# Waits between the gathers and the scatters that GpSimd issues in a routed expert layer

## The reference, cut to what matters

```python
xn = _layernorm(x, axis=-1)
x = x + attn_ref(xn, ...) + ffn_ref(xn, Wr, W1, W2)
...
# attn_ref: causal conv over 4 taps, two sigmoid gates, h = a*h + b along the sequence,
# a projection with W_out, and a root-mean-square norm
...
# ffn_ref: t = 4096 tokens, E = 8 experts, cap = 512 tokens each
eidx = jnp.argmax(probs, axis=-1)
...
keep = rank < cap
...
xe = xf[dispatch]
h = jnp.maximum(jnp.einsum('ecd,edf->ecf', xe, W1), 0.0)
ye = jnp.einsum('ecf,efd->ecd', h, W2)
ye = ye * (pe * valid)[:, :, None]
y = zeros.at[dispatch.reshape(-1)].add(ye.reshape(E * cap, d))
```

## Time and profile before

| what | us |
|---|---|
| median of 3 runs (lowest to highest) | 166.86 (165.87 to 166.94) |
| the profiled execution's own time | 165.59 |
| span of the profiled execution | 163.8 |
| POOL busy, of that in L350 and in L357 | 83.2, 32.1 and 37.1 |
| PE busy, DVE busy, ACT busy | 124.8, 93.5, 86.2 |

### The profile page before, as it was taken

The page is one execution under the profiler, slowest core; times in us unless marked ns, Lnnn a source line. Parts: engine busy times, 40 slices in busy tenths (PEclk is TensorE's granted clock), DMA queues, the critical chain, the costliest instruction groups (busy, mean ns, idle before and its releaser), DMA issues.

```text
span 163.8 us, 2058 instructions
## 1 busy us (share of the span) xinstructions
PE 124.8 (76%) x684; PEld 98.2 (60%) x684; DVE 93.5 (57%) x207; ACT 86.2 (53%) x197; POOL 83.2 (51%) x102
## 2 busy tenths in 40 slices
PE   5966999999995991699999739896979967941000
PEld 5956999836533890439659318694968956930000
DVE  4179300399898000861512410768948999299990
ACT  3047625014554840648685363999608958635650
POOL 7069640000477774377477876377765807560000
PEclk9997555579999999569999999999999999999555
DMA  4898699970011211011011111011110100116997
GB/s 133 231 270 315 268 356 342 399 318 2 16 48 36 54 58 48 18 49 49 16 52 48 48 48 48 16 50 49 49 46 21 33 16 32 42 58 183 327 301 214
DMA packets 14346, 19.27 MB, mean 118 GB/s; under 512 B 1664, under 2 KB 10112, under 8 KB 14336
## 3 DMA queue, kind: packets, MB, share of 16 engines
q1 hardware_dynamic: 9888, 13.63, 24.5%
q0 software_dynamic: 2048, 4.20, 8.7%
q10 hardware_dynamic: 2400, 1.32, 3.0%
HBM read 10.76 MB, written 8.39 MB: 117 GB/s over the span
## 4 chain that ended last, share of the span: by engine, by line
PE 40%; DVE 24%; DMA 8%; issue 8%; ACT 7%; another core or an unknown queue 6%; POOL 3%; POOLq 1%; SPq 0%; DVEq 0%; ACTq 0%
PE bank L495 8%; PE bank L427 7%; PE bank L385 7%; DVE xnT L869 5%; DMA x_tok<-in_x 4%; PE bank L395 4%; DVE xc L838 4%; PE bank L482 3%; DVE inp L865 3%; PE bank L416 3%; PE bank L484 2%; PE bank L483 2%; DVE dec L922 2%; DMA dec<-y_rows 2%
## 5 line engine op out<-in xcount | busy, mean ns | idle before, releaser
L357 POOL DMA_INDIRECT y_rows<-xn_tok,idx_out x32 | 37.1, 1159 | 25.2 <-DVE xn_tok L876 15.9
L350 POOL DMA_INDIRECT xn_tok<-xn_rows,idx_in x32 | 32.1, 1002 | 29.9 <-DVE idx_out L801 20.4
L618 ACT ACTIVATE h_sb<-bank 128x512 f32<-128x512 f32 x32 | 18.1, 596 | 25.7 <-PE bank L484 16.8
L495 PE MATMUL bank<-w_raw,h_sb 128*128 128x128 f32 x256 | 30.2, 275 | 0.1
L495 PEld LDWEIGHTS bank<-w_raw,h_sb 128*128 128x128 f32 x256 | 29.2, 192 | 0.2 <-issue 0.2
L482 PE MATMUL bank<-xg_hi,w_hi 128*128 128x512 f32 x32 | 14.0, 437 | 12.0 <-ACT h_sb L618 5.4
L427 PE MATMUL bank<-xc,par 128*128 128x512 f32 x32 | 17.2, 670 | 3.0 <-issue 2.8
L845 DVE TENSOR_TENSOR xg_lo<-bank,xg_hi 128x512 fp32r<-128x512 f32 x8 | 5.5, 688 | 18.6 <-ACT xg_hi L612 14.2
L876 DVE COPY xn_tok<-bank 128x512 f32<-128x512 f32 x7 | 4.8, 684 | 18.2 <-remote 11.3
L482 PEld LDWEIGHTS bank<-xg_hi,w_hi 128*128 128x128 f32 x32 | 6.1, 191 | 14.9 <-ACT h_sb L618 6.8
L427 PEld LDWEIGHTS bank<-xc,par 128*128 128x128 f32 x32 | 6.6, 214 | 12.0 <-issue 11.0
(11 more groups left out here) (111 smaller groups left out, 211.8 us busy)
## 6 DMA issues: line engine op xcount, KB each, us to landing
w_raw<-in_weights SPq DMA_DIRECT2D x8, 512.0 KB, 7.5
y_rows<-sca SPq DMA_DIRECT2D x4, 512.0 KB, 5.8
dec<-y_rows SPq DMA_DIRECT2D x8, 256.0 KB, 5.0
x_tok<-in_x SPq DMA_DIRECT2D x3, 512.0 KB, 9.4
xn_rows<-xn_tok SPq DMA_DIRECT2D x3, 512.0 KB, 3.5
out<-dec SPq DMA_DIRECT2D x4, 256.0 KB, 3.0
out<-dec ACTq DMA_DIRECT2D x4, 256.0 KB, 3.2
x_tok<-in_x SPq DMA_DIRECT2D x2, 256.0 KB, 5.4
```

The lines of the kernel that those rows point to most:

```text
L350: g.indirect_dma_start(gathered[:, s * D:(s + 1) * D], None, xn_rows, bass.IndirectOffsetOnAxis(ap=idx_in[:, s:s + 1], axis=0)).then_inc(g ...
L357: g.indirect_dma_start(y_rows, bass.IndirectOffsetOnAxis(ap=idx_out[:, s:s + 1], axis=0), gathered[:, s * D:(s + 1) * D], None).then_inc(s ...
L495: last = mm(tile_of(e, s), h_sb[:, k * CAP + s * P:k * CAP + (s + 1) * P], w_raw[:, e, F + k * D:F + (k + 1) * D], start=(k == 0), stop=(k ...
L618: a(h_sb[:, k * CAP:(k + 1) * CAP], hbank[n % 3][:, :], ACT.Relu).then_inc(h_done, 1)
```

## The change

GpSimd gets two waits in its loop over the experts. Ahead of each scatter it waits until the gather that it issued last has landed. Ahead of each gather in the loop it waits until all scatters so far have landed.

```diff
             pool.wait_ge(idx_done, 2)
             pool.wait_ge(zero_out, 16 * C)
+
             for e in range(E):
+                pool.wait_ge(gather_in[min(e + AHEAD, E) - 1], 16 * ST)
                 scatter(e)
                 if e + AHEAD < E:
+                    pool.wait_ge(scattered, 16 * ST * (e + 1))
                     gather(e + AHEAD)
```

## The result

The changed kernel took 168.3 us (167.7 to 169.9, 4 runs) beside 166.4 us of the kernel before: a ratio of 1.014, with a 95% interval of 1.010 to 1.019. It is slower by over 1%, inside the stated range but not in its likeliest case. The profiled execution took 168.28 us, with a span of 166.5. The chips turned out to be of two sorts: in three comparisons, this one included, the kernel before takes some 166 us, and in two, on two other chips, some 150.5 us.

What follows compares the result with a forecast made beforehand. PE (40% of the chain) and DVE (24%) set the end, POOL only 3%. Landings of 5.2 + 6.4 = 11.6 us fit into 12.0 us of room, so nothing is added: 166.9 us, range 164.7 to 170.2.

Steps and rivals of the forecast that it cites:

- likeliest case: The added waits stay hidden in GpSimd's idle time: 166.9 us, own range 166.0 to 168.2, chance 0.66.
- The cost of a turnaround: Ahead of gathers 4 to 7 and scatters 1 to 4: 1.30 us per scatter landing, 1.6 per gather landing, 11.6 in all.
- the upper bound for it: Gather 4's landing: DMA engines still move rows until 2.24 us after its descriptors are done; 1.6 us was taken.
- The room, and the walk through the loop: GpSimd's waits for DVE inside the loop leave 12.0 us to spend; start times forecast from gather 4 (74.6) to scatter 6 (135.6).
- slow stretch: Time in the chain without a known releaser while other engines stand still: 7.01 us from 59.12, 2.68 us from 120.65.
- Who waits for the later gathers: Gather 7 lands by 122.5, PE's transposes of it run at 126.74: 4.2 us of cover, more for gathers 4 to 6.
- PE's L469 should not wait for a gather: Sign in the profile after: PE's transposes of gathered rows are held by no gather.
- the start of scatter 7: Sign at the last expert: scatter 7 starts within 1 us of 141.7; after 143 the forecast is wrong.
- The rival that landings are longer: At the eight turnarounds, a surplus comes back eightfold: 0.5 us each gives 169.9 us; chance 0.24, other hold-ups included.
- The rival that stretches shrink: Waits break up the second stretch, at most 2.7 us: 164.2 us; with issue time at 94.38 gone too, 161.4; chance 0.10.
- The tail: SP's loads of `y_rows` behind scatter 7: the first 0.65 us of lateness are hidden, reserve about 1 us, beyond it all counts.
- theory C: From the experiments' expectations: PE's slow stretches set the end whatever the gathers do; 168 to 171 us for the early gather near 166.

Runs made afterwards that it cites:

- scatter_waits: The changed kernel with only the waits ahead of gathers 4 to 7: 156.21 us beside 150.67, ratio 1.037; again 155.75 us beside 150.29, ratio 1.036.
- gather_waits: The changed kernel with only the waits ahead of scatters, for the gather issued last: 157.8 us beside 150.67 of the kernel before, ratio 1.049.
- gather7_early: The changed kernel, both waits kept, but gather 7 right behind gather 6, ahead of scatter 3: 160.15 us beside 150.67 of the kernel before, ratio 1.064.
- gather7_early_no_waits: The kernel before, no added wait, but gather 7 right behind gather 6, ahead of scatter 3: 150.66 us beside 150.29, ratio 1.001.
- gather7_early_again: The changed kernel with gather 7 right behind gather 6, on another chip: 165.0 us beside 165.99 of the kernel before, ratio 0.998.

## Why the prediction was right, and where it was wrong

- **The cost of a turnaround.** Right. Forecast were 5.2 + 6.4 = 11.6 us on top of the usual 0.3 us gaps. Measured were 6.3 + 8.1 - 8 x 0.3 = 12.0 us: 1.27 us for a scatter's landing (1.30 taken) and 1.72 for a gather's (1.6 taken). The widest, gather 4's, took 2.54 - 0.30 = 2.24 us, as the upper bound for it had said. On the chips near 150.5 the total time puts 1.4 us on each, which includes that fewer DMAs were held up.
- **The room, and the walk through the loop.** Right for the profile it was read from, and POOL came to the last expert early. But the room of 12.0 us was taken as a property of the kernel. It depends on the chip: in four profiles from the other sort of chip (`scatter_waits`, `gather_waits`, `gather7_early`, `gather7_early_no_waits`), none with a slow stretch in its chain, GpSimd never waited for DVE longer than 0.3 us, so the room was zero. That the stretches make the room is argued from this, and from DVE's evictions coming 5.9 to 15.0 us earlier without them; no run takes them away and leaves the rest as it was.
- **Who waits for the later gathers.** This is the step that failed. I set gather 7's landing, forecast for 122.5, against PE's transposes at 126.74, and called the difference 4.2 us of cover. But 126.74 was where PE came because of slow stretches ahead of it, which I had named as a rival and left out of this step. In the changed kernel PE was there at 120.5, 2.0 us ahead of even the forecast landing, and the landing, 2.2 us later than forecast (the hold-ups of scatter 3), came at 124.67. A cover of 4.2 us became a stand of 4.2 us, followed by a lower clock that cost 2.4 us more. The sign that PE's L469 should not wait for a gather failed, and so did the start of scatter 7, at 144.30 instead of within 1 us of 141.7. `gather7_early_again` supports that this is the loss: without the stand it took 165.0 us, against 170.27 on the same chip. The evidence is not complete, as that kernel also has two turnarounds fewer and its twin without waits ran on the other sort of chip only.
- **The rival that landings are longer.** Its direction came true, not its mechanism: the landings were as forecast, and PE's wait for a gather ended last, not GpSimd's work. The upper end of the range, 170.2, was set by this rival, so that the range took the measured time in is in part luck.
- **The rival that stretches shrink.** Its first half came true: the stretch behind 120 and the issue time at 94 went, and PE ran 7.8 us ahead. The gain was lost again, to gather 7 (6.6 us with the clock) and to a new stretch behind 134 (3.7 us in the chain). That the waits as such cause or cure a stretch isn't shown: its place also moved with gather 7 alone.
- **The tail.** The last scatter started 148.09 - 145.52 = 2.6 us later and the span grew by 2.7 us. The 0.65 us of cover did not show: DVE's rows of the other branch, which come behind the last evictions and fill the tail, were late as well (first reciprocal at 146.14 instead of 143.38).

Against theory C as the cause stands `gather7_early_again`, which has a stretch of 7.0 us and lost nothing, though in the changed kernel the late stretch took its part of the lead. What makes PE slow in those stretches, and on some chips only, stays open. The changed kernel itself never ran on a chip near 150.5. No kernel run here beats the kernel before on either sort of chip; `gather7_early` equals it near 166 and costs 6% near 150.7.

## What to carry to other kernels

Idle time of an engine is room for a new wait only if whatever makes it idle is there on every chip and stays when the waits are in. Before counting on it, ask who makes the idle time, and try the kernel on more than one chip: near 166 us this change cost 2 to 3.4 us, or nothing where idle work held PE back, and near 150.5 parts of it cost 1.4 us per turnaround. And when the spare time between a transfer and its reader is used up, check it against the earliest time at which the reader could come, not against the time at which it came in one trace.

## What the runs showed of the hardware that was not expected

- The same kernel took 165.9 to 166.4 us in three comparisons and 150.3 to 150.7 us in two, on other chips. The difference builds up in three stretches in which PE's results come late against its own records (5.9, 3.9 and 2.8 us by DVE's evictions) and in the half clock behind the first (2.5 us). They lie at the same places within 0.1 us in two profiles of the kernel before and are absent from every chain read on the other chips.
- A landing as seen by GpSimd's wait: 1.27 us after the descriptors of a scatter, 1.5 to 2.2 us after those of a gather (gaps of 1.57 and 1.81 to 2.54 us, of which 0.3 us is the usual gap).
- After 4.18 us of standing, PE's next 32 matmuls took 6.13 us instead of 3.74, at a granted clock of 0.58 instead of 1.00. In the slow stretches the granted clock is 0.97 (59 to 66), 1.00 (120.6 to 123.3) and, in the changed kernel, 1.00 (135 to 142.7). Right behind the first it is 0.50. By the records it isn't the clock that makes them.
